# Conditional residual kernel: order of the opening loads, homes of the first prep tiles, order of TensorE's opening, and the bias rows as one table

## The reference, cut to what matters

```python
# layer 0: one of 64 weight matrices (512 x 512) and bias rows per block
x = x + einsum('bsd,bdh->bsh', x, W[cat_ids]) + b[cat_ids][:, None, :]
# layer 1: fc1 (512 -> 2048), gelu, fc2 (2048 -> 384 shared columns) and one of 16 experts (2048 -> 128 columns)
h = gelu(x @ fc1_w.T + fc1_b)
x = x + concat([h @ fc2_w.T + fc2_b, einsum('bnh,bph->bnp', h, experts_w[indices]) + experts_b[indices]], -1)
```

## Time and profile before

| | us |
|---|---|
| median of 3 runs | 1615.3 |
| lowest, highest | 1612.68, 1615.56 |
| the profiled execution | 1612.14 |
| its span, first to last instruction | 1610.3 |
| PE busy | 1598.0 (99%) |
| DVE busy | 1316.1 (82%) |
| ACT busy | 555.0 (34%) |
| POOL busy | 13.1 (1%) |

### The profile page before, as it was taken

The page is one execution under the profiler, slowest core; times in us unless marked ns, Lnnn a source line. Parts: engine busy times, 40 slices in busy tenths (PEclk is TensorE's granted clock), DMA queues, the critical chain, the costliest instruction groups (busy, mean ns, idle before and its releaser), DMA issues.

```text
span 1610.3 us, 28028 instructions
## 1 busy us (share of the span) xinstructions
PE 1598.0 (99%) x7096; PEld 1322.2 (82%) x7096; DVE 1316.1 (82%) x2192; ACT 555.0 (34%) x926; POOL 13.1 (1%) x17
## 2 busy tenths in 40 slices
PE   7999999999999999999999999999999999999999
PEld 6888888888888888888888888888888888888887
DVE  5988879788788888888888887887888888887865
ACT  4443333333333333333333333333333333333321
POOL 3000000000000000000000000000000000000000
PEclk8999999999999999999999999999999999999999
DMA  7765555555455555555555554555555545555410
GB/s 233 206 180 161 156 152 163 146 155 155 133 169 156 151 153 152 152 157 157 143 157 151 156 163 138 160 148 142 168 155 154 144 139 171 159 155 140 137 53 27
DMA packets 302335, 243.55 MB, mean 151 GB/s; under 512 B 34060, under 2 KB 234892, under 8 KB 302228
## 3 DMA queue, kind: packets, MB, share of 16 engines
q1 hardware_dynamic: 254180, 203.23, 44.5%
q10 hardware_dynamic: 48048, 39.35, 7.8%
HBM read 209.94 MB, written 32.51 MB: 151 GB/s over the span
## 4 chain that ended last, share of the span: by engine, by line
PE 98%; DVE 1%; DMA 0%; ACT 0%; issue 0%; DVEq 0%; POOL 0%; POOLq 0%
PE ps_out L910 43%; PE ps_h L878 22%; PE ps_e L878 22%; PE ps_y L870 11%; PE ps_t L819 1%; DMA e_blocks<-in_L_cond_fc_w 0%; PE ps_h L870 0%; PE ps_h L918 0%; PE ps_out L819 0%; DVE w2e L642 0%; DVE e_whole L705 0%; DVE resid L736 0%; PE ps_e L819 0%; ACT g_raw L560 0%; DVE h L642 0%
## 5 line engine op out<-in xcount | busy, mean ns | idle before, releaser
L910 PE MATMUL ps_out<-w2e,h 128*128 128x512 f32 x3072 | 736.6, 389 | 0.1
L910 PEld LDWEIGHTS ps_out<-w2e,h 128*128 128x128 f32 x3072 | 575.9, 188 | 119.4 <-DVE h L642 0.3
L878 PE MATMUL ps_h<-y_t,w 128*128 128x512 f32 (+1 forms) x1548 | 370.3, 388 | 0.0
L878 PE MATMUL ps_e<-y_t,w 128*128 128x512 f32 (+1 forms) x1548 | 370.3, 388 | 0.0
L878 PEld LDWEIGHTS ps_e<-y_t,w 128*128 128x128 f32 x1548 | 289.6, 188 | 59.5
L878 PEld LDWEIGHTS ps_h<-y_t,w 128*128 128x128 f32 x1548 | 289.3, 188 | 59.3
L546 ACT CAST w2e<-e_whole 128x512 fp32r<-128x512 f32 x256 | 158.7, 620 | 348.2 <-DVE e_whole L705 345.3
L705 DVE STREAM_TRANSPOSE e_whole<-e_blocks 128x512 f32<-128x512 f32 x256 | 277.1, 1082 | 0.0
L724 DVE CAST h<-g_raw 128x512 fp32r<-128x512 f32 x256 | 108.8, 425 | 162.5 <-ACT g_raw L560 158.6
L514 ACT CAST w_split<-w_raw 128x512 fp32r<-128x512 f32 x244 | 144.8, 620 | 190.6 <-DMA w_raw<-in_L_cond_W 96.2
L642 DVE TENSOR_TENSOR w2e<-e_whole,w2e 128x512 fp32r<-128x512 f32 x256 | 175.4, 685 | 18.1 <-ACT w2e L546 18.1
(11 more groups left out here) (76 smaller groups left out, 437.2 us busy)
## 6 DMA issues: line engine op xcount, KB each, us to landing
e_blocks<-in_L_cond_experts_w SPq DMA_DIRECT2D x1024, 64.0 KB, 2.5
w_raw<-in_L_cond_W SPq DMA_DIRECT2D x244, 256.0 KB, 3.9
out<-resid SPq DMA_DIRECT2D x64, 256.0 KB, 2.2
x_blocks<-in_x SPq DMA_DIRECT2D x240, 64.0 KB, 2.4
b_all<-in_L_cond_b SPq DMA_DIRECT2D x60, 256.0 KB, 4.2
x_raw<-in_x SPq DMA_DIRECT2D x60, 256.0 KB, 4.8
y_rows<-y ACTq DMA_DIRECT2D x60, 256.0 KB, 3.9
x_blocks<-y_rows ACTq DMA_DIRECT2D x240, 64.0 KB, 2.7
```

Of the source, the lines that this page charges most:

```text
L878: last = nc.tensor.matmul(h_bank(c)[:, at * S:end * S], w1[:, w, k, c * P:(c + 1) * P], y_t[:, a, k, at:end, :].rearrange("p b s -> p (b s)"),
L910: last = nc.tensor.matmul(ps_out[b][:, :], h[:, c % 2, a, b * S:(b + 1) * S], fc2_columns(c, c % 2, w, b), start=(c == 0 and n == 0), stop ...
```

## The change

- Slices are loaded one by one, with a semaphore each. All four bias rows follow the first two slices. Prep tile 0 is loaded after slice 8, the others after slice 15, all by SP; expert pieces are put between the last slices and prep loads. ACT issues only x 0, x 1 and b1 at the start.
- Six prep tiles have homes of their own (PSLOTS 3 -> 2, OWN_PREP = 6), outside the experts' buffer.
- The bias rows come as one table of 8 rows; POOL makes the halves of all in one pass, and a selecting matrix `row_of` picks the block's two rows in the matmul.
- The four engines' opening lists are rewritten: `keep_busy` 12, 6 and 8 in place of 6; no prep turn ahead of the slices; prep 5 and 6 are turned in the loop behind fc1 of step 0.

```diff
-    FIRST_W = ((0,), (1,), (2,), (3,), (4, 5), (6, 7), (8, 9), (10, 11), (12, 13), (14, 15))
-    PSLOTS = 3
+    PSLOTS = 2
+    OWN_PREP = 6
@@ SP
+            def load_first_w(j):
+                after(sp, w_lo, w_lows(0, j - W0SLOTS))
+                src = l0_w[bass.ds(first_cats[j // KD], 1), :, :].rearrange("o (p k) n -> k (o p) n", k=KD)[j % KD]
+                sp.dma_start(w_slot(0, j), src).then_inc(w0_in[j], 16)
...
+            first_cats = [category(0, 0)]
+            load_first_w(0)
+            load_first_w(1)
+            for b in range(GB):
+                if b > 0:
+                    first_cats.append(category(0, b))
+                load_b0_row(b)
+            for j in range(2, 6):
+                load_first_w(j)
+            load_first_x(2)
+            for j in range(6, 9):
+                load_first_w(j)
+            load_prep(sp, 0)
+            load_first_w(9)
+            load_first_w(10)
+            load_first_x(3)
             sp.wait_ge(exps_in, 16)
             first_experts = [index(exps, b, exp_w.shape[0]) for b in range(GB)]
-            load_experts(0, 0, first_experts, range(GB))
+            for j in range(11, NC):
+                load_first_w(j)
+                if j < NC - 1:
+                    load_experts(0, 0, first_experts, [0], [j - 11])
+            for t in range(1, QUAD):
+                load_prep(sp, t)
+                load_experts(0, 0, first_experts, [t])
+            for t in range(QUAD, OWN_PREP + PSLOTS):
+                load_prep(sp, t)
@@ POOL
+            pool.wait_ge(b0_rows_in, 16 * GB)
+            nc.gpsimd.tensor_scalar(b0_high, b0_rows, row_sign[0:2 * GB, 0:1], None, ALU.mult).then_inc(b0_high_ready, 1)
+            pool.wait_ge(b0_high_ready, 1)
+            nc.gpsimd.tensor_tensor(b0_halves, b0_high.bitcast(F32), b0_rows, ALU.add).then_inc(b0_ready, 1)
@@ ACT
             x_high(0, 0)
-            load_prep(act, 2)
-            load_prep(act, 3)
-            prep_high(0)
-            prep_high(1)
             w_high(0, 0)
             w_high(0, 1)
             x_high(0, 1)
             for j in range(2, 6):
                 w_high(0, j)
-            load_prep(act, 4)
-            prep_high(2)
+            y_high(0, 0)
             w_high(0, 6)
             w_high(0, 7)
-            y_high(0, 0)
             x_high(0, 2)
             w_high(0, 8)
             w_high(0, 9)
-            load_prep(act, 5)
-            prep_high(3)
+            y_high(0, 1)
+            prep_high(0)
             w_high(0, 10)
             w_high(0, 11)
-            load_prep(act, 6)
-            y_high(0, 1)
             x_high(0, 3)
             w_high(0, 12)
             w_high(0, 13)
-            prep_high(4)
+            y_high(0, 2)
             w_high(0, 14)
             w_high(0, 15)
-            y_high(0, 2)
+            prep_high(1)
+            y_high(0, 3)
+            prep_high(2)
+            prep_high(3)
+            prep_high(4)
             prep_high(5)
-            y_high(0, 3)
-            prep_high(6)
@@ ACT, step c of the loop
                     gelu(g, c)
+                    if first(g) and c == 0:
+                        prep_high(6)
@@ DVE, the new list (lines that stay and lines that are new)
             x_low(0, 0); w_low(0, 0); w_low(0, 1); x_low(0, 1); w_low 2, 3, 4
             y_sum(0, 0); w_low(0, 5); w_low(0, 6); y_low(0, 0); w_low(0, 7); x_low(0, 2); w_low(0, 8)
             y_sum(0, 1); w_low(0, 9); w_low(0, 10); y_low(0, 1); prep_low(0); w_low(0, 11); x_low(0, 3); w_low(0, 12)
             y_sum(0, 2); w_low(0, 13); w_low(0, 14); y_low(0, 2); w_low(0, 15); prep_low(1)
             y_sum(0, 3); y_low(0, 3); prep_low(2); prep_low(3); turn_e(0, 0); prep_low(4); prep_low(5)
@@ DVE, step c of the loop
                     h_high(g, c)
+                    if first(g) and c == 0:
+                        prep_low(6)
@@ PE
+            keep_busy(12)
+            turn_x(0)
             keep_busy(6)
-            turn_x(0)
-            turn_prep(0)
-            turn_prep(1)
             turn_x(1)
-            turn_prep(2)
-            turn_prep(3)
-            for j in range(6):
+            keep_busy(8)
+            for j in range(5):
                 l0_slice(0, j)
             turn_y(0)
+            l0_slice(0, 5)
             l0_slice(0, 6)
             turn_x(2)
             l0_slice(0, 7)
             l0_slice(0, 8)
-            turn_prep(4)
+            turn_prep(0)
+            turn_y(1)
             l0_slice(0, 9)
-            turn_y(1)
+            l0_slice(0, 10)
             turn_x(3)
-            for j in range(10, 14):
-                l0_slice(0, j)
+            l0_slice(0, 11)
+            l0_slice(0, 12)
             turn_y(2)
+            l0_slice(0, 13)
             l0_slice(0, 14)
-            turn_prep(5)
             l0_slice(0, 15)
+            turn_prep(1)
             fc1_ahead(0, range(KD // 2))
             turn_y(GB - 1)
+            turn_prep(2)
             fc1_ahead(0, range(KD // 2, KD))
-            turn_prep(6)
+            turn_prep(3)
+            turn_prep(4)
             fc1_ahead(1, range(KD))
@@ PE, step c of the loop
                     fc1(g, c)
+                    if first(g) and c == 0:
+                        turn_prep(5)
+                        turn_prep(6)
```

More of the change, by code:

```diff
@@ L98, in build @@
         e_whole = sb("e_whole", [P, GB * P])
[L99 to L102, removed]
+        b0_rows = y[0:2 * GB, GB - 1, :]
+        b0_high = w2e[0:2 * GB, W2_SIZE - 2 * D:W2_SIZE - D]
+        b0_halves = w2e[0:2 * GB, W2_SIZE - D:W2_SIZE]
+        row_of = w1[0:2 * GB, 1, KD - 1, HID - GB * P:HID]
         y_hold = w_raw[:, WSLOTS:WSLOTS + 2, :]
@@ L120, in build @@
         prep_in = [sem(f"prep_in{i}") for i in range(PSLOTS)]
-        first_prep_in = [sem(f"first_prep_in{t}") for t in range(QUAD)]
-        w0_in = [sem(f"w0_in{i}") for i in range(len(FIRST_W))]
+        first_prep_in = [sem(f"first_prep_in{t}") for t in range(OWN_PREP)]
+        w0_in = [sem(f"w0_in{j}") for j in range(NC)]
         w_in = [sem(f"w_in{i}") for i in range(WSLOTS)]
@@ L129, in build @@
         b0_in = sem("b0_in")
-        b0_rows_in = [sem(f"b0_rows_in{b}") for b in range(GB)]
+        b0_rows_in = sem("b0_rows_in")
         be_in = sem("be_in")
@@ L201, in prep_bank @@
             return ps_out[t % GB] if t < PREP_FIRST else ps_t
[L203 to L205 removed]
         def prep_tile(t):
[L209 to L211 removed]
+            if t < OWN_PREP:
+                return (prep_raw[:, 0, :], prep_raw[:, 1, :], be_all[:, :, :].rearrange("p b n -> p (b n)"), b0_all[:, :],
+                        g_raw[:, 1, :], x_raw[:, :])[t]
+            return prep_raw[:, t % PSLOTS, :]
         def prep_earlier(t):
[L215 removed]
+            return [u for u in range(OWN_PREP, t) if u % PSLOTS == t % PSLOTS]
         def prep_later(u):
[L219 removed]
+            return [t for t in range(OWN_PREP + PSLOTS, NPREP) if max(prep_earlier(t)) == u]
         def prep_dst(t, half):
@@ L329, in load_prep @@
         def load_prep(eng, t):
-            if t < QUAD:
+            if t < OWN_PREP:
                 eng.dma_start(prep_tile(t), prep_src(t)).then_inc(first_prep_in[t], 16)
                 return
-            after(eng, prep_turned, max(prep_earlier(t), default=-1) + 1)
-            eng.dma_start(prep_tile(t), prep_src(t)).then_inc(prep_in[prep_slot(t)], 16)
+            eng.wait_ge(prep_turned, t % PSLOTS + 1 if t < OWN_PREP + PSLOTS else max(prep_earlier(t)) + 1)
+            eng.dma_start(prep_tile(t), prep_src(t)).then_inc(prep_in[t % PSLOTS], 16)
         @block.sync
@@ L384, in load_b0 @@
                 after(sp, xb_ready, (G - 1) * GB + b)
+                if first(G - 1) and b == 0:
+                    sp.wait_ge(prep_turned, OWN_PREP)
                 sp.dma_start(b0_all[:, :], l0_b[bass.ds(cat, 1), :].to_broadcast([P, D])).then_inc(b0_in, 16)
@@ L422, in load_expert_bias @@
                 after(sp, resid_ready, g * GB)
+                if first(g):
+                    sp.wait_ge(prep_turned, OWN_PREP)
                 for b in range(GB):
@@ L486, in _ @@
                                     base=0, pattern=[[-1, P]], channel_multiplier=1).then_inc(ident_ready, 1)
[L488 to L491, removed]
-            pool.wait_ge(row_sign_ready, 1)
[L493 to L500, removed]
+            nc.gpsimd.memset(row_of.bitcast(F32), 0.0).then_inc(row_of_zeroed, 1)
+            nc.gpsimd.memset(row_sign[0:2 * GB, 0:1], -1.0).then_inc(row_sign_set, 1)
+            pool.wait_ge(row_of_zeroed, 1)
+            for n, done in enumerate((row_of_high, row_of_ready)):
+                if n == 1:
+                    pool.wait_ge(row_of_high, 1)
+                nc.gpsimd.affine_select(out=row_of.rearrange("p (b m) -> p b m", b=GB),
+                                        in_=row_of.bitcast(F32).rearrange("p (b m) -> p b m", b=GB),
+                                        compare_op=ALU.not_equal, fill=1.0, base=-n * GB,
```

(41 more changed lines are left out.)

36 lines of the change are left out of this document (9 added, 27 removed).

## The result

The changed kernel took 1624.45 us (median of 4 runs, 1624.25 to 1628.03), the kernel before 1615.02 beside it (1612.68 to 1615.56): ratio 1.0066, 95% interval 1.0049 to 1.0084. It is slower by 0.66%, which is the forecast sign, and 0.45 us above the top of the range. The sign came for the reasons given (the middle and the end took longer, as walked); the size is wrong. The forecast was +3.9 us, the medians differ by 9.4, the profiled executions by 12.1 (span 1622.4 against 1610.3).

The account below looks back on a forecast made before the run. TensorE was taken to bound the loop, so only the first fc2's start counts: the middle gives back the opening's 5.5 us, then 1.5 + 2.4 = +3.9 us, 1615.3 + 3.9 = 1619.2 us; range 1611 to 1624.

Parts of the forecast that it names:

- The start of layer 0: Opening: after 52 keep_busy records, half price once the clock rises, layer 0 starts at 10.5 us, 3.2 earlier.
- The middle: y_sum(0) at 14.05 to y_sum(3) at 36.5: rounds of 6.8, 7.9 and 7.8 us give back the 5.5 gained, 0.7 more.
- The end: From y_sum(3) at 36.5 to the first fc2 at 48.15: first fc1's end +1.5 us, moved prep tiles +2.4.
- the moved pair: Prep 5 and 6 in loop step 0 stand ahead of gelu and h_low: fc2 +2.4 us, bounds 0 and 3.0.
- Casts queued behind a y_high that waits for TensorE: Middle, ACT: y_high(0) stands ahead of slice 6's cast, so ACT waits for the turned y until 15.6 us.
- prep_low(1) ahead of y_sum(3): VectorE, end of the middle: prep 1's cast ends at 35.9, so y_sum(3) starts at 36.5 against 35.84 before.
- the supply term: Opening: SP through with bias rows at about 7.2 us; W2 lands in 2.5, split by 11.2, in time for slice 2.
- (a): Rival: half clock comes back through TensorE's idle gaps in the walk of 15 to 36 us; +2.9, 1622.1; chance 0.14.
- (b): Rival: low first clock level lasts through all keep_busy calls, layer 0 starts at 14.8, 4.2 later, 1623.4; chance 0.06.
- (c): Rival: middle rounds shorter than walked, a third of their 8.7 us excess goes; 2.9 less, 1616.3, no change; chance 0.18.
- (d): Rival: TensorE's own opening work, 24.4 us, is the bound; fc2 at 39.3, -4.9, 1610.4; chance 0.14.
- The claim that a shift at the first fc2 goes through to the end one for one: Loop behind the first fc2: a shift of h_low reaches the kernel's end in full, here +3.9 us.

Follow-up runs that it names:

- rows_form: Changed kernel with bias rows again as pairs on neighbouring partitions, one POOL pass per block, same place; 1624.04 us, 1.0063 of the kernel before.
- rows_next: Changed kernel, bias table kept, but each row's two copies on neighbouring partitions 2b and 2b + 1; 1623.73 us, 1.0044 of the kernel before.
- order: Changed kernel with ACT, VectorE and TensorE lists of the middle in the old order, without early prep turns; 1622.01 us, 1.0043 of the kernel before.
- order_tail: Changed kernel with the old middle order and prep 5 and 6 ahead of the loop, loads and table as changed; 1619.22 us, 1.0032 of the kernel before.
- all3: order_tail with bias rows as pairs, each issued among its block's loads, keep_busy 12, 6, 8; 1612.5 us, 0.9990 of the kernel before.
- all3_kb: all3 with keep_busy 6, 8, 4 in place of 12, 6, 8; 1613.82 us, 0.9998 of the kernel before.
- tail: Changed kernel with prep 5 and 6 turned and split ahead of the loop again; 1625.2 us, 1.0061 of the kernel before.

## Why the prediction was right and where it was wrong

**Right.** The start of layer 0 (10.5, measured 10.48), with keep_busy at half its first price. The middle: walked 22.4 us, measured 22.98 with a half clock stretch in it, and 22.41 in rows_form and rows_next, which had full clock there; from y_sum to y_sum it was 7.31, 7.81 and 7.86 for the 6.8, 7.9 and 7.8 walked. The end: walked 11.7, measured 11.80; within it the moved pair, whose removal gained 1.34 where 1.5 was reckoned. Of the mechanisms named, prep 5 and 6 ahead of the gelu are shown by undoing them alone. Casts queued behind a y_high that waits for TensorE and prep_low(1) ahead of y_sum(3) were undone together, in order; the timeline gives 1.7 us to the second (1.6 walked).

**Wrong.** The failing step is the supply term, what four bias rows and three reads cost SP: "SP is through with the rows at about 7.2, and W2 to W4 go out at 7.2, 7.7 and 8.1." Slice 2 went out at 10.84, 3.64 late. Of this 0.6 was my addition: the terms in the text, 3.8 + four times 0.29 + three times 0.96, make 7.8. Another 0.4 or 0.5 are not in these terms, since with neighbouring partitions, at the prices taken, slice 2 went out at 8.27 and 8.35. The other 2.5 is the price that I took over from rows with two neighbouring partitions: a row cost 0.65 to 0.79 instead of 0.29 and the read behind it 0.73 instead of 0.49, once the copies lay four partitions apart. Slices 2 and 3 then landed after 3.2 and 4.1, not 2.5. And TensorE, idle from 12.1 to 15.46, fell to half clock, which cost 1.1 us ahead of y_sum(0). Together y_sum(0) came 5.36 us later than walked, which is nearly all of the 6.0 by which the first fc2 was missed. Undoing it is worth 4.05 us at the first fc2 in rows_form, and with the place 7.3 there and 6.7 in the time between order_tail and all3. In rows_form itself the gain at the first fc2 does not show in the time, and why is open.

**The rivals.** (a), half clock again, happened from 15.5 to 22.4, but behind the wait for the late loads and not in the walk's gaps. In rows_form and rows_next, where that wait is shorter, it fell on the first fc2 instead; the walk's gaps may have brought it on, which no run tried. (b), slow keep_busy throughout, is refuted by 1.50 us for 12 records. (c), shorter rounds, is refuted by 22.41. (d), TensorE's own work as the bound with fc2 at 39.3, did not hold even in all3 (42.40). The point that should decide for (d), ACT casting slice 6 before y_sum(0) is done, was not met in the changed kernel (22.02 and 20.10). In order it was (18.94 and 19.56), and the middle still had waits.

**The end.** The claim that a shift at the first fc2 goes through to the end one for one holds only roughly. For seven of the ten kernels the shift of fc2 against the kernel before lies within the interval of the time (9.97 in 7.9 to 13.6 us for the changed one). For order, rows_form and all3_kb the time is worse than that: 4.38 for 4.8 to 9.2, 5.92 for 7.4 to 12.9, and -2.36 for -1.8 to 1.1. From the first fc2 to the span's end it was 1566.1 before, 1568.2 changed, 1570.5 in rows_form, 1573.1 in all3_kb; TensorE's scattered waits (0, 1.3, 2.5 and 4.8 us) and a half clock stretch behind fc2 (1.6) bring these down to 1566.1 to 1568.3. Why these waits differ was not tried. The profiled execution of before had none, and lay 3.2 us below its median.

## What to carry to other kernels

Take an issuing queue's price for a transfer from a row with the same destination pattern, and add up what the queue does between two loads before trusting "the queue is empty": an idle DMA queue is a warning, not a gain. When a list in program order is rewritten, walk it: an engine's wait for a round trip (sum, turn, cast) holds everything listed behind it. Independent casts and sums listed ahead of such waits, on three engines together, were worth 5.3 us here. Work moved "into the loop" costs nothing only if it stands behind the loop's own chain on each engine, not ahead of it.

## What the runs showed of the hardware that I had not expected

A DMA that copies one 2 KB row to two partitions took SP 0.28 us to issue when the partitions were neighbours and 0.66 (0.79 the first time) when they were four apart, and the register read behind it went from 0.49 to 0.73 us. Why was not tried. The clock's half speed lay elsewhere in each profile of an opening: 8 to 19 us, 15 to 22, 31 to 42, 50 to 54 or nowhere. Small changes of the opening are not all of it, since executions of one kernel differ too: of 46 of the kernel before, timed beside the experiments, the mean granted clock was from 0.995 to 1.000. It was not free where TensorE waits a lot: 1.1 us ahead of y_sum(0) (changed against tail), 1.5 between y_sum(2) and y_sum(3) (order_tail against order), and 1.6 on the first fc2 for 12 matmuls.
